# An RWKV time mix and six attention nodes on one core: k's moves held until rows of maxima are stored, later projections, unit 0 in half steps

## What is computed

```python
x = x + time_mix(layernorm(x))        # x is [4, 1024, 128]: k, v, r projections, a scan over time, sigmoid gate, Wo
nodes = {-1: layernorm(x)}
for c in range(6):
    nsrc = min(c + 1, 5)
    q = ew[c, 0] * (nodes[c - 1] @ We[eq] + be[eq])
    k = ew[c, 1] * (nodes[c - nsrc] @ We[ek] + be[ek])
    v = ew[c, 2] * (nodes[c - nsrc + nsrc // 2] @ We[ev] + be[ev])
    o = mha(q, k, v, Wq[c], Wk[c], Wv[c], Wo[c])      # 8 heads of 16, softmax over 1024 keys
    nodes[c] = act_w[c] * o + q
x = x + layernorm(nodes[5]) * g + b
```

## Time and profile before

| | us |
|---|---|
| median of 3 runs (lowest, highest) | 2377.87 (2376.58, 2405.42) |
| the profiled execution | 2382.87 |
| its span, first to last instruction | 2381.0 |
| mean granted clock of TensorE | 0.971 |

### The profile page before, as it was taken

The page is one execution under the profiler, slowest core; times in us unless marked ns, Lnnn a source line. Parts: engine busy times, 40 slices in busy tenths (PEclk is TensorE's granted clock), DMA queues, the critical chain, the costliest instruction groups (busy, mean ns, idle before and its releaser), DMA issues.

```text
span 2381.0 us, 43523 instructions
## 1 busy us (share of the span) xinstructions
PE 2247.4 (94%) x16493; PEld 905.9 (38%) x16493; DVE 2069.2 (87%) x3260; ACT 1795.6 (75%) x3432; POOL 529.2 (22%) x667
## 2 busy tenths in 40 slices
PE   7998999999999999999999999999999999999998
PEld 3533333343333333343333333333333333334333
DVE  6878899898999988998988988989889879889896
ACT  4366787787787877887877877878778778778776
POOL 4330320222312202212202112112022022321213
PEclk9989999999999999999999999999999999999999
DMA  4230322323314314224223223134033132331301
GB/s 130 57 64 21 78 58 57 78 59 71 76 38 91 66 34 87 56 60 87 57 49 79 62 54 76 35 73 85 23 79 74 32 80 52 71 76 44 66 24 50
DMA packets 87535, 149.37 MB, mean 63 GB/s; under 512 B 35146, under 2 KB 49950, under 8 KB 87326
## 3 DMA queue, kind: packets, MB, share of 16 engines
q0 software_dynamic: 28224, 94.13, 18.9%
q1 hardware_dynamic: 59102, 52.46, 8.8%
HBM read 42.36 MB, written 14.91 MB: 24 GB/s over the span
## 4 chain that ended last, share of the span: by engine, by line
PE 69%; DVE 17%; DMA 10%; issue 2%; SPq 1%; ACT 1%; POOL 0%; DVEq 0%; POOLq 0%; ACTq 0%
PE context L646 26%; PE ring L601 24%; DMA rows_dram<-max_turn 8%; PE wide L625 8%; DVE max_neg L1234 8%; DVE max_neg L1231 6%; PE wide L527 2%; PE wide L516 2%; PE wide L508 2%; DMA q_aug<-rows_dram 2%; PE wide L536 1%; PE wide L541 1%; PE context L471 1%; DVE max_all L1240 1%; DVE max_part L1245 1%
## 5 line engine op out<-in xcount | busy, mean ns | idle before, releaser
L877 ACT ACTIVATE e_ring<-ring 128x512 f32<-128x512 f32 x3054 | 1603.2, 600 | 421.6 <-PE ring L601 419.7
L1231 DVE TENSOR_REDUCE max_neg<-wide 128x1 f32<-128x512 f32 x1816 | 1145.2, 682 | 184.6 <-PE wide L625 183.6
L625 PE MATMUL wide<-k_aug,q_aug 48*128 48x512 f32 x3072 | 1089.1, 448 | 42.0 <-DVE max_neg L1231 33.1
L601 PE MATMUL ring<-q_aug,k_aug 50*128 50x512 f32 x3054 | 1048.5, 441 | 57.8 <-DMA q_aug<-rows_dram 56.3
L646 PE MATMUL context<-e_ring,v_aug 128*32 128x256 f32 (+1 forms) x9168 | 922.9, 475 | 0.6 <-ACT raw L886 0.6
L1234 DVE TENSOR_REDUCE max_neg<-wide 128x2 f32<-128x1024 f32 x628 | 762.3, 1218 | 59.4 <-PE wide L625 58.5
L601 PEld LDWEIGHTS ring<-q_aug,k_aug 50*128 50x128 f32 x3054 | 501.7, 189 | 773.4 <-ACT e_ring L877 593.9
L625 PEld LDWEIGHTS wide<-k_aug,q_aug 48*128 48x128 f32 x3072 | 508.7, 188 | 95.8 <-DVE max_neg L1231 64.1
L646 PEld LDWEIGHTS context<-e_ring,v_aug 128*32 128x32 f32 x9168 | 182.1, 109 | 417.9 <-issue 281.4
L381 POOL DMA_DIRECT2D src<-node_dram x40 | 22.9, 571 | 719.2 <-PE wide L527 719.2
L1335 POOL CAST q_part<-q_part 128x512 fp32r<-128x512 f32 x46 | 28.1, 611 | 453.6 <-ACT q_part L846 440.0
(11 more groups left out here) (240 smaller groups left out, 957.5 us busy)
## 6 DMA issues: line engine op xcount, KB each, us to landing
q_aug<-q_part POOLq DMA_DIRECT2D x138, 256.0 KB, 4.7
k_aug<-k_part POOLq DMA_DIRECT2D x138, 256.0 KB, 7.1
src<-node_dram POOLq DMA_DIRECT2D x40, 512.0 KB, 7.0
ctxT<-raw SPq DMA_DIRECT2D x380, 32.0 KB, 2.0
rden_bc<-rden_dram SPq DMA_DIRECT2D x23, 512.0 KB
node_dram<-node_ring SPq DMA_DIRECT2D x16, 512.0 KB, 2.9
q_aug<-rows_dram SPq DMA_DIRECT2D x192, 8.0 KB
node_ring<-in_L_attn_x SPq DMA_DIRECT2D x4, 512.0 KB, 4.9
```

Source lines behind the costliest of these rows:

```text
L601: e.matmul(bk[:, :], k_aug[first:first + AUG, u % 2, h // 2, chunk * P:(chunk + 1) * P].bitcast(F32R), q_aug[first:first + AUG, u % 2, h / ...
L625: e.matmul(bk[:, :], q_aug[first:first + SPLIT, u % 2, head // 2, q0:q0 + P].bitcast(F32R), k_aug[first:first + SPLIT, u % 2, head // 2, h ...
L877: e.activation(e_ring[:, n % E_SLOTS, :], bank[where["st", n]][:, :], ACT.Exp, scale=EXP_SCALE).then_inc(a_exp, 1)
L1231: e.tensor_reduce(max_neg[:, G % 2, kh, row:row + 1], wide[:, b, :], AX_X, ALU.max, negate=True).then_inc(v_mx, 1)
```

## The change

k's six moves stand two steps later and, at r=12, wait on d_rows, the semaphore of the rows' store of the same step; src's load at r=28 waits likewise. The tables K_AT, OUT_AT, TURN_AT, V_AT and Q_AT move by two steps, with q's moves (r=5 to 10), normalise (r=10) and the spill (r=21). The reciprocal stands at the start of r=8, its store at r=8 and its spread at r=9. v is evicted at the start of the step after its projection. In units whose previous one is final, POOL's affine stands at r=28. Unit 0 keeps the old steps for k, v and takes q at steps 2 and 3; its loop goes one step at a time, with products and mixing stages both in ring banks. The output projection of the last but one unit keeps its steps.

```diff
-        K_AT, OUT_AT, TURN_AT, V_AT, Q_AT = (5, 9), (13, 17), 19, (21, 25), (29, UC + 1)
+        K_AT, OUT_AT, TURN_AT, V_AT, Q_AT = (7, 11), (15, 19), 21, (23, 27), (31, UC + 3)
+        FIRST_K_AT, FIRST_V_AT, FIRST_Q_AT, LAST_OUT_AT, LAST_TURN_AT = (5, 9), (21, 25), (2, 3), (13, 17), 19
...
             if u + 1 < LAST:
-                return (20, 23), (21, 24), (22, 25), 27, 31
+                return (22, 25), (23, 26), (24, 27), 28, 31
...
             first = UC * (u - 2)
-            return (first + Q_AT[0], first + Q_AT[1]), first + UC + 3
+            return (first + Q_AT[0], first + Q_AT[1]), first + UC + 5
...
-            for s in range(0, ALONE, 2):
+            for s in range(0, UC):
+                made = products(s)
                 pair(s, 0)
                 pair(s, 1)
-                if s > 0:
+                for kind, unit, hf in made:
+                    product(kind, unit, hf, next_bank())
+                if s > 0 and not made:
+                    weighted(s - 1, first_half, True, False)
+                pair(s, 2)
+                pair(s, 3)
+                if made:
+                    weighted(s - 1, whole, True, True)
+                elif s > 0:
+                    weighted(s - 1, second_half, False, True)
+                mix_at(s)
+
+            for s in range(UC, ALONE, 2):
...
-                    if half == 1 and r == 3:
-                        for kind in range(2):
-                            e.wait_ge(d_den[kind], DMA * (GPU // 2) * (prev + 1))
-                        if prev > 0:
-                            e.wait_ge(d_rden_out, DMA * NHALF * prev)
-                        e.reciprocal(rden_pack[:, :], den_pack[:, :]).then_inc(v_rec, 1)
...
+            def before_maxima(s):
+
+                u, r = divmod(s, UC)
+                nxt, prev = u + 1, u - 1
+                if 1 < nxt < UNITS and r - 1 in V_AT:
+                    evict_v(nxt, V_AT.index(r - 1))
+                if 0 <= prev < LAST and r == 8:
...
+                    e.reciprocal(rden_pack[:, :], den_pack[:, :]).then_inc(v_rec, 1)
...
+            def wait_rows_stored(s):
+
+                for G in finished(s):
+                    e.wait_ge(d_rows[G % 2], DMA * (G // 2 + 1))
+
...
-                    if r == 26:
+                    if r == 28:
+                        wait_rows_stored(s)
                         load_source(e, nxt + 1, 0)
...
-                if 0 <= prev < LAST and (r, half) == (8, 1):
+                if 0 <= prev < LAST and (r, half) == (10, 1):
                     normalise(prev)
...
-                    if r == 10:
-                        e.wait_ge(p_st, HG * s)
+                    if r == 12:
+                        wait_rows_stored(s)
                         for n in range(K_MOVES // 2):
                             move_k(e, nxt, n)
...
-                if 1 <= nxt < UNITS and half == 0 and r == 11:
+                if 1 <= nxt < UNITS and half == 0 and r == 13:
...
-                        if r == 4:
+                        if r == 8:
                             store_rden(prev)
-                        if r == 5:
+                        if r == 9:
                             spread_rden(prev)
-                        if r == 19 and CELLS[prev][0] < SPILLED:
+                        if r == 21 and CELLS[prev][0] < SPILLED:
                             spill(prev)
```

More of the change, by code:

```diff
@@ L276, in q_steps, with k_steps, v_steps, out_steps @@
         def q_steps(u):
-            if u in (1, 2):
-                first = UC * (u - 1)
-                return (first + 3, first + 3), first + 5
+            if u == 1:
+                return FIRST_Q_AT, 5
+            if u == 2:
+                return (UC + 3, UC + 3), UC + 5
             first = UC * (u - 2)
-            return (first + Q_AT[0], first + Q_AT[1]), first + UC + 3
+            return (first + Q_AT[0], first + Q_AT[1]), first + UC + 5
+        def k_steps(u):
+            return FIRST_K_AT if u == 1 else K_AT
+        def v_steps(u):
+            return FIRST_V_AT if u == 1 else V_AT
+        def out_steps(u):
+            return (OUT_AT, TURN_AT) if u < LAST - 1 else (LAST_OUT_AT, LAST_TURN_AT)
         def products(s):
@@ L289, in products @@
             if 1 <= nxt < UNITS:
-                found += [("k", nxt, hf) for hf in range(2) if r == K_AT[hf]]
-                found += [("v", nxt, hf) for hf in range(2) if r == V_AT[hf]]
+                found += [("k", nxt, hf) for hf in range(2) if r == k_steps(nxt)[hf]]
+                found += [("v", nxt, hf) for hf in range(2) if r == v_steps(nxt)[hf]]
             for unit in (nxt, nxt + 1):
@@ L295, in products @@
             if 0 <= prev < LAST:
-                found += [("out", prev, hf) for hf in range(2) if r == OUT_AT[hf]]
-                if CELLS[prev][0] == NODES - 1 and r == TURN_AT:
+                found += [("out", prev, hf) for hf in range(2) if r == out_steps(prev)[0][hf]]
+                if CELLS[prev][0] == NODES - 1 and r == out_steps(prev)[1]:
                     found += [("turn", prev, hf) for hf in range(2)]
@@ L328, in build @@
             taken += HG
-            if s >= 0 and s % 2 == 1:
+            if s >= UC and s % 2 == 1:
                 taken += len(products(s))
@@ L656, in pair, with product @@
                     maxima(h)
-            def product(kind, unit, hf):
+            def product(kind, unit, hf, at):
                 make = {"k": head_k, "q": head_q, "v": project_v, "out": project_out, "turn": final_turn}[kind]
-                make(unit, hf, next_max_bank())
+                make(unit, hf, at)
             def mix_at(s):
@@ L734, in tensor_program @@
                 for kind, unit, hf in products(s + 1):
-                    product(kind, unit, hf)
+                    product(kind, unit, hf, next_max_bank())
                 weighted(s, first_half, True, False)
@@ L927, in scalar_program @@
                     fold(FOLDS_AT.index(s) + 1)
-            for s in range(0, ALONE, 2):
+            for s in range(0, UC):
+                for k in range(HG):
+                    exponential(s, k)
+                    if k == 1:
+                        for kind, unit, hf in products(s):
+                            evict(kind, unit, hf)
+                mix_at(s)
+                if s > 0 and s % NCH == 0:
+                    evict_context(s // NCH - 1)
+            for s in range(UC, ALONE, 2):
                 for k in range(HG):
@@ L932, in scalar_program @@
                 exponential(s + 1, 0)
-                if s > 0 and s % NCH == 0:
+                if s % NCH == 0:
                     evict_context(s // NCH - 1)
@@ L1159, in stages @@
                 nxt, prev = u + 1, u - 1
-                if 1 <= nxt < UNITS:
-                    if half == 1 and r in V_AT:
-                        evict_v(nxt, V_AT.index(r))
+                if nxt == 1 and half == 0 and r in FIRST_V_AT:
+                    evict_v(nxt, FIRST_V_AT.index(r))
                 if 0 <= prev < LAST:
-                    if half == 1 and r == 3:
-                        for kind in range(2):
-                            e.wait_ge(d_den[kind], DMA * (GPU // 2) * (prev + 1))
-                        if prev > 0:
-                            e.wait_ge(d_rden_out, DMA * NHALF * prev)
-                        e.reciprocal(rden_pack[:, :], den_pack[:, :]).then_inc(v_rec, 1)
                     if CELLS[prev][0] == NODES - 1:
@@ L1205, in stages @@
                     last_affine(1)
+            def before_maxima(s):
[4 more added lines that the diff above has]
+                if 0 <= prev < LAST and r == 8:
+                    for kind in range(2):
+                        e.wait_ge(d_den[kind], DMA * (GPU // 2) * (prev + 1))
+                    if prev > 0:
+                        e.wait_ge(d_rden_out, DMA * NHALF * prev)
+                    e.reciprocal(rden_pack[:, :], den_pack[:, :]).then_inc(v_rec, 1)
             for t in range(TURNS):
```

11 lines of the change are left out of this document (7 added, 4 removed).

## The result

| | before | after |
|---|---|---|
| median us (lowest, highest; runs) | 2383.81 (2376.58, 2405.42; 4) | 2244.66 (2242.01, 2254.19; 4) |
| ratio after/before, 95% interval | | 0.9409 [0.9339, 0.9480] |
| profiled execution, its span | 2382.87, 2381.0 | 2245.28, 2243.5 |
| mean granted clock | 0.971 | 0.994 |

The account below looks back on a forecast made before the run. The bound was taken as PE and DVE standing still together, at PE's 56.3 us of waits for q_aug's rows. 78.9 + 5 = 84 us off the 2377.87 median, 2 given back, gave 2296 us, range 2268 to 2345.

Parts of the forecast that it names:

- k's moves held the store: k's moves slow the rows' store at r=12; holding them gains 78.9 us over 22 stretches, r=12 to r=20.
- The undisturbed stretch: One unit's quick-store stretch, r=12 to r=20: 23.1 us, DVE time 19.70 plus 3.4, taken for all.
- a sign (23 to 24.5): If right, r=12 to r=20 stretches would last 23 to 24.5 us at granted clock 1.00.
- The new wait itself is free: POOL reaches k's moves after rows are stored, no cost; t0 is the issue of the rows' store at r=12.
- v's projection ... I cost it at nothing; k, q and out keep their four steps of distance: Moving the projections two steps costs nothing; half reductions in units 1 to 23 keep their number.
- Final units, 5 us gained: POOL's affine at r=28 no longer stalls DVE's first split: two units at 2.4 us, say 5 us.
- Unit 0, taken as 0 with bounds -12.6 to +7: Half steps in unit 0: clock might return 12.6 us, smaller context matmuls might cost 7; 0 taken.
- Rival A: Normalise on POOL stalls DVE's split at r=12, 2.2 us in each of 22 units, 48 us: 2344; chance 0.17.
- B: k's moves slow the rows' load after r=12 instead, 1 us in 22 units: about 2318; chance 0.10.
- C: Spread slows the rows' store and k's moves then slow its load, 110 us slower: 2488; chance 0.05.
- D: The spread slows the rows' store to 9.0 us, load stays quick, waits remain: 2378; chance 0.08.
- My sign "under 5 us of waits for q_aug's rows": If right, PE's waits for the rows of maxima in q_aug would fall from 56 us to under 5.

Follow-up runs that it names:

- the moves alone: Kernel before with only k's six moves put at r=12 and 13, behind the wait for the stored rows: 2287.18 us, ratio 0.9558.
- The experiment that puts three kinds back: Changed kernel with the projections of k, v and q back at their old steps, out staying moved: 2290.27 us, ratio 0.9575.
- The two runs with v alone: Kernel before with k's moves behind the stored rows, and v's projections at r=23, 27 or at r=19, 23: 2279.25 and 2284.84 us.
- the repeat of the moves alone: Kernel before with only k's moves at r=12 and 13 behind the stored rows, run again: 2285.64 us, ratio 0.9550.

## Why the prediction came out wrong

The direction and the main cause hold; the size does not: 2296 forecast, 2244.66 measured, outside 2268 to 2345. By its steps:

- **k's moves held the store: right, undersized.** Store to load 9.0 to 2.0 us; PE's wait and the low clock go. Forecast 78.9 us, measured alone 92.5. The undisturbed stretch was taken as DVE's time plus 3.4 us, one case for all. With the moves alone the 22 stretches last 512.8 us with DVE busy for 446.5: 66.3 over, 3.0 each. DVE's own time fell by 5.5 more. The rest is that the earlier trace rows cut by SP's stores, 612.6 us against 605.3 from split to split. My own range for the term, 72 to 95, held it. The median stretch was 23.0 us with the moves alone, as I had named it for a sign (23 to 24.5), and 21.55 in after, where the projections act too.
- **"The new wait itself is free": right.** Without it the time is the same. Normalise (t0+1.2 forecast, t0+0.8 to 1.8 in most units), k's first move (t0+5.5 forecast, 5.9 to 7.5 but for the two units with a collision) and the landing of k (at most 10.4 us after issue) all kept their margins; no maxima waited for k_aug. My t0+5.5 had left out POOL's 0.56 us ahead of the first move: by my own terms it is t0+6.0.
- **"v's projection ... I cost it at nothing; k, q and out keep their four steps of distance": this is the step that failed.** The distance from one projection to the next stays, as I wrote, and so does the number of half reductions outside unit 0. The distance from the projection to DVE's split does not. Moving all of them puts PE's 1.1 us or more without maxima just ahead of DVE's 0.7 us without reductions: 87 waits become 5, and some 2 us a unit go. The experiment that puts three kinds back prices it at 45 us, 27.0 of them in the stretches from r=28 to 12, where after gained 31.4. Of these 31.4, 5.6 lie behind the slow split of unit 20 (next point). The two runs with v alone bear out the mechanism by their waits, and its size only in part. I had compared how the instructions of one engine stand to each other, and not what the other engine does at that moment.
- **Final units, 5 us gained: the mechanism is right, its size depends on the clock.** The slow splits at r=28 of units 20 (2.31 us) and 22 (1.74 us) are gone in after. They are still there with the moves alone: the stretches behind them, to r=4, last 26.8 and 25.7 us there at granted clock 0.87 and 0.80, and 21.4 and 19.5 at 1.00 in the kernel with three projections back. Without the reciprocal that left them (1.1 us) that makes 10.5 us. In the repeat of the moves alone they last 25.2 and 21.3 us at 0.93 and 1.00, which makes 4.6. I had counted the hold and not the clock behind it.
- **Unit 0, taken as 0 with bounds -12.6 to +7: wrong, -16.** The count of eight fewer reductions was right (142 DVE instructions to 134), my 2.2 us for smaller context matmuls were not what decided, and the lower bound was too near: I had allowed only the clock to come back. The stretch from r=4 to 12 went from 33.8 to 29.1 us at granted clock 1.00 in both.
- **Rival A (normalise meets the split) came true in 3 units of 23**, for 8.5 us, not in all and not in none. The rule of the Trainium skill that I had set beside it (GPSIMD Engine Reference, Key points) agrees: the split's instructions have two SBUF inputs. Reductions from PSUM went on undisturbed: in unit 7 those beside normalise took 1.28 us for two halves and 1.22 for a whole one, as elsewhere.
- **Rivals B, C and D: not seen.** Beside normalise's spread the store took 2.0 us in most units and 3.1 at most.
- **Missed: the later output projection holds SP.** I had checked who waits for that projection's result, but not who waits until its input may be overwritten. SP stood 421.8 us in all at that wait (221.6 before), and the store of r=20 stood behind it: 15.2 us of PE's waits, 17.5 us of the stretches from r=20 to 28. My sign "under 5 us of waits for q_aug's rows" failed because of this, not because of k.

By the two traces the change gave 137.5 us where 84 was forecast. Of the 53.5 us between, 13.6 are the main term (92.5 for 78.9), 16.0 unit 0, 31.4 the stretches from r=28 to 12 and 16.7 what r=12 to 20 gives beyond the moves alone (109.2 for 92.5). The slower r=20 to 28 takes 20.7 back, the two ends give 1.9, and the 5 us of the final units, which lie within these rows, are to be taken off: 53.9, up to rounding.

## What to carry to other kernels

When two engines feed each other in lock step and each has work of its own, put the work of one that holds up the other just ahead of the other's own: moving the projections by two steps took away 82 of 87 such waits. When a producer is moved, read every in-order queue that waits for it, also those that only wait to overwrite its input, and look at what small urgent issue stands behind that wait. A bulk transfer that isn't wanted soon belongs behind the small store that is.

## What the runs showed of the hardware

- A store of 16 KB took 9.0 us in unit 7 of before while six moves of 256 KB, issued by another engine, were in flight (8.3 to 11.6 in 21 of the units 1 to 22), and 2.0 us when they were held. Most of it is waiting, not slow transfer: the first of its 128 packets began 5.4 us after the issue, its packets took 2.3 us, and the load went out 1.3 us later; in after these are 1.2, 0.4 and 0.4 us. In the first 5.3 us k's packets took, by the profile, all of the 16 DMA engines' time (101%), and no packet of the store is among them. Beside the spread of 512 KB it took 2.0 us, so it was not the mere presence of a transfer. The Trainium skill says (DMA: Bandwidth & Descriptors, on arbitration) that a DMA engine takes turns between its queues, and drains a whole packet of some 9 to 17 descriptors from one before it switches. A long wait ahead of the first packet fits that, but no run here shows how long a turn was.
- Short waits of PE cost more than themselves. In unit 2 of after PE stood 1.51 us behind the slow split, and the stretch has a granted clock of 0.94, part of it at 1.2 GHz; with the slow split and that wait gone the stretch is 2.9 us shorter at 1.00.
- The hold of DVE by a POOL TENSOR_TENSOR lasts as long as the POOL instruction: 2.38 us for one of 2.39 that had begun 0.04 us earlier.
